# Row gathers moved behind the branch, the first tile's pairs moved ahead, first scores put inside the projections

## What is computed

```python
def rgcn(h, V, w_comp, loop_w, bias, ffn_w, ffn_b, ln_g, ln_b, norm, src, dst, etype):
    Hb = einsum('ni,bio->bno', h, V)                 # 4 bases
    coef = w_comp[etype]
    m = sum(coef[:, b][:, None] * Hb[b][src] for b in range(4)) * norm[:, None]
    agg = segment_sum(m, dst)
    hn = relu(agg + h @ loop_w + bias)
    y = hn @ ffn_w.T + ffn_b + h
    return (y - mean(y)) / sqrt(var(y) + 1e-8) * ln_g + ln_b

def conv(x, src, dst, Wq, bq, Wk, bk, Wv, bv, Ws, bs):   # 2 heads of 64
    q, k, v = x @ Wq + bq, x @ Wk + bk, x @ Wv + bv
    alpha = sum(q[dst] * k[src], -1) / 8
    a = segment_softmax(alpha, dst)
    return segment_sum(v[src] * a, dst) + x @ Ws + bs

x = layernorm(x + rgcn(x, ..., edge_weight, src, dst, edge_type))
x = layernorm(x + conv(relu(conv(x, ...1)), ...2))
```

## Time and profile before

| | us |
|---|---|
| median of 3 runs (range) | 2037.31 (2036.69 to 2038.35) |
| the profiled execution, its own time | 2049.78 |
| its span in the trace | 2047.9 |
| start to the first pair product (L842) | 51.6 |
| second block ends, layer 1 begins | 1078.9 |
| layer 2 begins | 1563.2 |

### The profile page before, as it was taken

The page is one execution under the profiler, slowest core; times in us unless marked ns, Lnnn a source line. Parts: engine busy times, 40 slices in busy tenths (PEclk is TensorE's granted clock), DMA queues, the critical chain, the costliest instruction groups (busy, mean ns, idle before and its releaser), DMA issues. The chain is left out here.

```text
span 2047.9 us, 53122 instructions
## 1 busy us (share of the span) xinstructions
PE 1958.0 (96%) x19165; PEld 1634.9 (80%) x19165; DVE 1438.9 (70%) x4141; ACT 1287.0 (63%) x2275; POOL 663.0 (32%) x802
## 2 busy tenths in 40 slices
PE   1699999999999999999998999999998999999998
PEld 1599999999999999999985777777776677777777
DVE  4787878777887877778635666666664666776665
ACT  1476766767676676767654666666663666666665
POOL 3566576566657656665310000000000000000000
PEclk8799999999999999999999999999999999999999
DMA  3012111111211111121013222222211232222220
GB/s 82 6 38 76 41 39 49 67 39 39 73 44 39 47 69 39 39 73 40 34 66 125 70 91 94 94 93 70 88 63 64 99 103 94 79 98 101 101 101 8
DMA packets 43019, 137.00 MB, mean 67 GB/s; under 512 B 9191, under 2 KB 24360, under 8 KB 36485
## 3 DMA queue, kind: packets, MB, share of 16 engines
q1 hardware_dynamic: 38484, 128.24, 17.5%
q0 software_dynamic: 4400, 6.80, 1.4%
HBM read 91.83 MB, written 43.20 MB: 66 GB/s over the span
## 5 line engine op out<-in xcount | busy, mean ns | idle before, releaser
L854 PE MATMUL ps<-matrixT,x_rows 125*128 125x256 f32 (+1 forms) x2500 | 563.6, 377 | 0.1
L1670 DVE CUSTOM_DVE_ANT_0 scores_l<-ps,bias_rows_l 125x500 f32<-125x500 f32 (+1 forms) x700 | 396.7, 619 | 212.6 <-issue 212.6
L854 PEld LDWEIGHTS ps<-matrixT,x_rows 125*128 125x128 f32 x2500 | 461.3, 190 | 48.5 <-issue 0.2
L1575 ACT COPY weightsT_l<-ps 125x500 f32<-125x500 f32 x400 | 229.7, 575 | 289.0 <-PE ps L1502 288.4
L942 ACT COPY matrixT<-ps 125x500 f32<-125x500 f32 (+2 forms) x800 | 381.8, 658 | 45.8 <-PE ps L842 44.4
L1502 PEld LDWEIGHTS ps<-eye,scores_l 125*125 125x125 f32 x2500 | 287.9, 188 | 118.2 <-issue 105.1
L842 PE MATMUL ps<-high_weights,low_onehot 64*125 64x125 f32 x6300 | 373.9, 274 | 5.2 <-DVE high_weights L722 3.3
L842 PEld LDWEIGHTS ps<-high_weights,low_onehot 64*125 64x125 f32 x6300 | 358.5, 187 | 24.1 <-issue 18.5
L1567 ACT ACTIVATE scores_l<-scores_l,neg_max_l 125x1500 f32<-125x1500 f32 x200 | 318.0, 1594 | 20.6 <-DVE neg_max_l L1705 20.6
L1502 PE MATMUL ps<-eye,scores_l 125*125 125x125 f32 x2500 | 325.2, 281 | 4.0 <-ACT weightsT_l L1575 2.7
L1487 PE MATMUL ps<-kT_l,q_tile_l 64*125 64x500 f32 (+1 forms) x1400 | 319.1, 567 | 6.6 <-DVE chunk_max_l L1670 4.8
(11 more groups left out here) (152 smaller groups left out, 1600.5 us busy)
## 6 DMA issues: line engine op xcount, KB each, us to landing
bias_rows_l<-bias SPq DMA_DIRECT2D x50, 1562.5 KB, 6.6
bias<-bias SPq DMA_DIRECT2D x75, 500.0 KB
x_rows<-in_x SPq DMA_DIRECT2D x1, 1562.5 KB
bias<-bias SPq DMA_DIRECT2D x25, 62.5 KB
x<-x_rows SPq DMA_DIRECT2D x25, 62.5 KB
x_rows_l<-x SPq DMA_DIRECT2D x25, 62.5 KB
out<-rows_l SPq DMA_DIRECT2D x25, 62.5 KB
dst_int<-in_dst SPq DMA_DIRECT2D x1, 402.8 KB
```

The costliest lines, as they stand in the source:

```text
L854: last = nc.tensor.matmul(psG[:, BASES * SPLIT * side:BASES * (SPLIT * side + SIDE[side])], x[:, h, :], MT[side][:, 0:SIDE[side], BASES * ...
L1575: nc.scalar.copy(PT[i][:, 0:cw[c]], psT[i % 3][0:R, 0:cw[c]]).then_inc(z["pa_ok"], 1)
L1670: V.tensor_tensor_reduce(S[par][:, hd, lo:hi], psS[2 * ((par + j) % 2) + hd][0:R, 0:cw[j]], bias[par][0:R, lo:hi], 1.0, FLOOR, ALU.add, AL ...
```

## The change

There are three parts. The gathers of the rows of tiles 0 and 1 leave the first block and stand at the head of GpSimd's list in the second. In step 3 of the second block the second side of tile 0's pair products (and ScalarE's evacuation of it) stands ahead of the turning of tile 1's edge weights instead of behind it. In both attention layers ScalarE evacuates k as well as q; the projections of q and k use PSUM banks 4 to 7, so that banks 0 to 3 are free for scores; tile 0's scores stand between and behind the projections of q and k; and the values come after them, in one row over four banks, with their evacuation on VectorE behind tile 0's masks and negative maximum.

```diff
@@ -284,8 +284,6 @@
                                     pattern=[[-1, 128]], channel_multiplier=1).then_inc(const, 1)
             nc.gpsimd.memset(m["spare"][:, :], 0.0).then_inc(const, 1)
             pool.wait_ge(const, 5)
-            for s in range(EARLY):
-                find_row(nc, pool, a, m, s, s)
 
         @block.tensor
         def _(pe):
@@ -549,6 +547,8 @@
 
         @block.gpsimd
         def _(pool):
+            for s in range(EARLY):
+                find_row(nc, pool, a, m, s, s)
             nc.gpsimd.memset(half_power[:, :], -0.5).then_inc(const, 1)
             pool.wait_ge(const, 1)
 
@@ -890,13 +890,16 @@
                     turn_digits(w + 1, par)
                 if inside(u):
                     sums(u, 1, 3)
+                if w == 0:
+                    pair_products(w, 1)
                 if inside(w + 1):
                     read(u, 3)
                     pe.wait_ge(digitsT_ok, w + 2)
                     turn_codes(w + 1, par)
 
                 if inside(w):
-                    pair_products(w, 1)
+                    if w > 0:
+                        pair_products(w, 1)
                     sums(w, 0, 0)
                 if inside(w + 1):
                     pe.wait_ge(codesT_ok, w + 2)
@@ -991,6 +994,8 @@
                 if inside(u):
                     logs(u, 3)
                     sums_out(u, 1)
+                if is_int(w) and w == 0:
+                    evacuate(w, 1)
                 if inside(w + 1):
                     act.wait_ge(codes_ps, w + 2)
                     turned = psM[:, :].rearrange("p (b n) -> p n b", n=128)
@@ -1000,7 +1005,8 @@
                     last.then_inc(codesT_ok, 1)
 
                 if inside(w):
-                    evacuate(w, 1)
+                    if not is_int(w) or w > 0:
+                        evacuate(w, 1)
                     for piece in range(PIECES):
                         counts_out(w, 0, piece)
                 if is_int(w) and w == 0:
@@ -1375,6 +1381,7 @@
         groups = [(g, min(4, T - g)) for g in range(0, T, 4)]
         cw = widths()
         psS, psT, psO = ps[0:4], ps[4:7], ps[7]
+        psQ = ps[4:8]
         ORDER = (0, 1, 2, 3, 4, 5, 6, 7, 8, 12, 13, 9, 10, 11)
         ON_V, ON_A = (1, 4, 7, 10), (0, 2, 3, 5, 6, 8, 12, 9, 11)
         NT = HEADS * CH
@@ -1423,7 +1430,7 @@
         def _(pool):
             nc.gpsimd.memset(half_power[:, :, :], -0.5).then_inc(z["one"], 1)
             pool.wait_ge(z["one"], 1)
-            pool.wait_ge(z["q_ok"], CH)
+            pool.wait_ge(z["q_ok"], 1)
 
             def lay_q(t, par):
 
@@ -1432,6 +1439,7 @@
                 nc.gpsimd.tensor_copy(q_now[par][:, :], qT[:, bass.ds(t * R, R)]).then_inc(z["q_laid"], 1)
 
             lay_q(0, 0)
+            pool.wait_ge(z["q_ok"], CH)
 
             def step(t, par):
                 if inside(t + 1):
@@ -1447,23 +1455,25 @@
 
         @block.tensor
         def _(pe):
-            for j in range(CH):
+            pe.wait_ge(z["one"], 1)
+
+            def project(j):
+
                 if j >= 2:
                     pe.wait_ge(z["q_ok"], j - 1)
                     pe.wait_ge(z["k_ok"], j - 1)
-                nc.tensor.matmul(ps[j % 2][:, 0:cw[j]], W["q"][:, :], inT[:, CW * j:CW * j + cw[j]], start=True, stop=True).then_inc(z["q_ps"], 1)
-                nc.tensor.matmul(ps[2 + j % 2][:, 0:cw[j]], W["k"][:, :], inT[:, CW * j:CW * j + cw[j]], start=True, stop=True).then_inc(z["kk_ps"], 1)
+                nc.tensor.matmul(psQ[j % 2][:, 0:cw[j]], W["q"][:, :], inT[:, CW * j:CW * j + cw[j]], start=True, stop=True).then_inc(z["q_ps"], 1)
+                nc.tensor.matmul(psQ[2 + j % 2][:, 0:cw[j]], W["k"][:, :], inT[:, CW * j:CW * j + cw[j]], start=True, stop=True).then_inc(z["kk_ps"], 1)
+
+            def values(j):
+
                 g, k = groups[j]
-                if j >= 2:
-                    pe.wait_ge(z["v_ok"], j - 1)
+                if j >= 4:
+                    pe.wait_ge(z["v_ok"], j - 3)
                 for i in range(k):
-                    to = ps[4 + j % 2][0:R, i * D:(i + 1) * D]
+                    to = psQ[j % 4][0:R, i * D:(i + 1) * D]
                     last = nc.tensor.matmul(to, inT[:, (g + i) * R:(g + i + 1) * R], W["v"][:, :], start=True, stop=True)
                 last.then_inc(z["v_ps"], 1)
-            pe.wait_ge(z["q_ok"], CH)
-            pe.wait_ge(z["k_ok"], CH)
-            pe.wait_ge(z["v_ok"], len(groups))
-            pe.wait_ge(z["one"], 1)
 
             def product(u, c):
 
@@ -1479,6 +1489,8 @@
             def scores(t, par, j):
                 if j == 0:
                     pe.wait_ge(z["q_laid"], t + 1)
+                if is_int(t) and t == 0:
+                    pe.wait_ge(z["k_ok"], j + 1)
 
                 if not is_int(t) or t * CH + j >= 2:
                     pe.wait_ge(z["masked"], (t * CH + (j - 2)) * 2 + 2)
@@ -1506,11 +1518,29 @@
                 for i in range(lo, hi):
                     turn(u, up, i)
 
+            def first_step():
+
+                for j in range(CH):
+                    project(j)
+                    if j in (3, 5):
+                        scores(0, 0, j - 3)
+                        scores(0, 0, j - 2)
+                for j in range(4, CH):
+                    scores(0, 0, j)
+                pe.wait_ge(z["q_ok"], CH)
+                for j in range(len(groups)):
+                    values(j)
+
             def step(t, par):
                 u, up, w = t - 1, 1 - par, t - 2
+                if is_int(t) and t == 0:
+                    first_step()
+                    return
                 if inside(t):
                     scores(t, par, 0)
                     scores(t, par, 1)
+                if is_int(t) and t == 1:
+                    pe.wait_ge(z["v_ok"], len(groups))
                 if inside(u):
                     turns(u, up, 0, 3)
                 if inside(w):
@@ -1548,8 +1578,11 @@
             act.wait_ge(z["bq_ok"], 1)
             for j in range(CH):
                 act.wait_ge(z["q_ps"], j + 1)
-                nc.scalar.activation(qT[:, CW * j:CW * j + cw[j]], ps[j % 2][:, 0:cw[j]], ACT.Identity, scale=SCALE,
+                nc.scalar.activation(qT[:, CW * j:CW * j + cw[j]], psQ[j % 2][:, 0:cw[j]], ACT.Identity, scale=SCALE,
                                      bias=bq_scaled[:, :]).then_inc(z["q_ok"], 1)
+                act.wait_ge(z["kk_ps"], j + 1)
+                nc.scalar.activation(kT[:, CW * j:CW * j + cw[j]], psQ[2 + j % 2][:, 0:cw[j]], ACT.Identity,
+                                     bias=bk[:, :]).then_inc(z["k_ok"], 1)
 
             def sums_out(w, par):
                 act.wait_ge(z["pv_ok"], (w + 1) * CH)
@@ -1605,14 +1638,14 @@
             V = nc.vector
             V.memset(qT[:, NODES:NODES + R], 0.0)
             V.tensor_scalar_mul(bq_scaled[:, :], bq[:, :], SCALE).then_inc(z["bq_ok"], 1)
-            for j in range(CH):
-                v.wait_ge(z["kk_ps"], j + 1)
-                V.tensor_scalar_add(kT[:, CW * j:CW * j + cw[j]], ps[2 + j % 2][:, 0:cw[j]], bk[:, :]).then_inc(z["k_ok"], 1)
-                g, k = groups[j]
-                v.wait_ge(z["v_ps"], j + 1)
-                V.tensor_tensor(vals[:, g:g + k, :, :], ps[4 + j % 2][0:R, 0:k * D].rearrange("p (t h f) -> p t h f", h=HEADS, f=HD),
-                                bv.rearrange("p (h f) -> p h f", h=HEADS).unsqueeze(1).to_broadcast([R, k, HEADS, HD]),
-                                ALU.add).then_inc(z["v_ok"], 1)
+
+            def values_out():
+                for j in range(len(groups)):
+                    g, k = groups[j]
+                    v.wait_ge(z["v_ps"], j + 1)
+                    V.tensor_tensor(vals[:, g:g + k, :, :], psQ[j % 4][0:R, 0:k * D].rearrange("p (t h f) -> p t h f", h=HEADS, f=HD),
+                                    bv.rearrange("p (h f) -> p h f", h=HEADS).unsqueeze(1).to_broadcast([R, k, HEADS, HD]),
+                                    ALU.add).then_inc(z["v_ok"], 1)
 
             def finish(w, par, then):
                 v.wait_ge(z["exp_ok"], (w + 1) * 4)
@@ -1703,6 +1736,8 @@
                     if not is_int(t) or t >= 2:
                         v.wait_ge(z["exp_ok"], (t - 1) * 4)
                     V.tensor_scalar_mul(neg[par][:, :], top[:, :], -1.0).then_inc(z["neg_ok"], 1)
+                if is_int(t) and t == 0:
+                    values_out()
                 if inside(u):
                     turned_out(10)
                 if layer == 2 and inside(w):
```

## The result

| | kernel before | changed kernel |
|---|---|---|
| median of 4 runs (range), us | 2037.83 (2036.69 to 2038.86) | 2026.82 (2025.05 to 2030.42) |
| ratio, 95% interval | | 0.9947 (0.9933 to 0.9962) |
| profiled execution, us | 2049.78 | 2030.42 |

The change gives 11 us (8 to 14 by the interval), where 27.7 were forecast; the time lies 10 us above the top of the range. Measured again later, the changed kernel took 2029.32 beside 2037.88, ratio 0.9955 (0.9941 to 0.9968).

A forecast was written before the change was run, and what follows sets the result against it. TensorE was taken as the bound, with time to win only where it waits. Gathers 7.2, second side 8.6 and attention layers 11.9 sum to 27.7 us off 2037.31, giving 2009.6; range 2005.5 to 2016.5, chance 0.59.

The forecast's parts named there:

- every engine's branch and its first instructions move along: End of first block: with the barrier 7.5 us earlier, all engines' starts behind it come earlier too; 7.2 us taken.
- the time that VectorE takes to come out of its branch: Start of second block: this time hides GpSimd's constant ahead of the first wait; VectorE wants first rows at 21.1.
- the barrier stays: Rival, end of first block: drain is the barrier's own time or engines wait for code; gain 0, 2016.8 us, chance 0.04.
- gathers late: Rival, start of second block: moved gathers meet x and weights and land late; gain 3.5 us, 2013.3, chance 0.13.
- after that VectorE waited for TensorE in the old order and has this time to give: Second block after unit 3 of tile 1: VectorE's slack (20% idle) lets TensorE's 8.6 us gain stand.
- Slower: Rival, second block: VectorE, working beside GpSimd's coefs every step, becomes the bound; 55 us lost, 2064.8, chance 0.04.
- nothing in VectorE's row after it is longer than before: Second block after unit 3: argument against the rival that only VectorE's own 2.2 us is won.
- new gaps after 100 us: Sign of being wrong: TensorE shows new gaps in the second block's steps after 100 us.
- VectorE gates: Rival, step 3 of second block: unit 3 or the logarithms come after TensorE; only 2.2 us won, 2016.0, chance 0.08.
- 1.75 for the clock: Start of each attention layer: first projection chunk takes 1.75 us more at the lower clock, counted in old and new order.
- with no waits 6.6 each: Attention layers: upper bound of the reordering's gain, 6.6 us in each layer if TensorE never waits.
- projections worth less: Rival, attention layers: ScalarE's pitch or late bias rows leave 4 us a layer; 2013.5 us, chance 0.11.

The follow-up runs named there:

- part 3 alone: Kernel before with only the attention reordering (scores inside the projections, both layers); 2030.69 us, ratio 0.9965.
- x_late: Changed kernel with SyncE asking for x after all weights, in the second block; one execution, 2040.52 us, total not meaningful since x is late.
- x112: Changed kernel with x loaded as 112 and 13 partitions instead of 125; 2035.83 us beside 2050.9, ratio 0.9930; repeated 2021.44, ratio 0.9925.
- p23_x112: Changed kernel with x loaded as 112 and 13 partitions and the gathers back in the first block; 2035.08 us beside 2050.9, ratio 0.9920.
- best: Changed kernel with x and destination loads split by partitions, four logarithm tiles, bias fills on GpSimd; 2028.87 us beside 2050.9, ratio 0.9895; repeated 2013.88, ratio 0.9884.
- ln4: Changed kernel with four tiles for ScalarE's logarithms, one for each piece, instead of two; 2024.11 us beside 2038.99, ratio 0.9931.
- part 2 alone: Kernel before with only tile 0's second side put ahead of tile 1's weights; 2034.19 us, ratio 0.9981.
- parts 2 and 3: Changed kernel with the row gathers put back in the first block; 2024.24 us, ratio 0.9941 against the kernel before.
- p1_only: Kernel before with only the gathers moved to the second block; 2040.2 us beside 2037.84, ratio 1.0011.
- x_split: Changed kernel with x asked for on two queues, 13 tiles by SyncE and 12 by ScalarE; 2028.21 us beside 2038.99, ratio 0.9946.
- p23_best: Kernel with split x and destination loads, four logarithm tiles and GpSimd's fills, but gathers in the first block; 2015.9 us, ratio 0.989.

## Why the prediction was wrong, point by point

**The forecast's frame held.** TensorE stays busy through the steady steps, and what a start gains arrives at the end: part 3 alone, 7.1 by the medians, 7.7 read off the layers. All three sizes were too large: 27.7 forecast, 9 to 11 measured. The lower bounds missed too: their sum was 13.2, part 1 (3) and part 3 (8) fell below theirs, and only part 2 came out above its 2.2.

**Part 1, forecast 7.2, measured -2.2.** The failed step is "every engine's branch and its first instructions move along". The branch moved; the first instructions did not. The prediction took "the time that VectorE takes to come out of its branch" (5.1 us before, counted from the end of the reading of the flag) as a fixed length, but it is 8.1 us with x in flight and 3.3 to 3.7 without (x_late, x112, p23_x112 and both forms of best). The price lay in the rows: GpSimd issues at 16.0 was put in from 23.54 - 7.5, while x was named only as something that "does not come earlier" and as a risk for the gathers' landing, never for the starts. The rival "the barrier stays" held the right words, "or all engines wait for code", at a chance of 0.04, and argued against only the first half. The rival "gathers late" was right that the landing is the drain's 5.6 us under x, but priced it behind an issue at 19.5 that came at 26.4. Behind the late start the gathers now stand in front, which turned nothing into a loss of 2.2. Even with x out of the way the step gives about 1 us, since it puts issue and landing behind the branch that had run inside the drain.

**Part 2, forecast 8.6, measured 3.9.** Up to the place where the forecast stopped its sum it was right: 9.07 us read (40.56 against 49.63). The failed step is "after that VectorE waited for TensorE in the old order and has this time to give". It priced the units alone. In step 4 VectorE has two fills and four bias rows besides, in the old order too. It comes to the first of them 56.9 us after the first pair product (111.02), where it was 62.6 before (114.27): 5.8 us earlier, while TensorE is 9.1 earlier. The rows that carry this are, in the kernel before,

```profile
103.33 0.55 DVE L717 TENSOR_TENSOR high_weights<-iota,digitsT 128x200 f32<-128x200 f32 x1 [6.00 <-PE ps L842]
...
114.27 0.89 DVE L735 MEMSET bias<- 32x1000 f32 x1 [0.26 <-issue]
```

and in the changed one

```profile
98.03 0.62 DVE L717 TENSOR_TENSOR high_weights<-iota,digitsT 128x200 f32<-128x200 f32 x1
...
111.02 0.89 DVE L735 MEMSET bias<- 32x1000 f32 x1 [0.26 <-issue]
```

VectorE's wait of 6.0 us is used up. And counted from the first pair product it starts on these units 7.8 us earlier (43.87 against 51.69), but loses 2.05 of that before the fill: 12.99 us against 10.94. All three of its units now lie beside GpSimd's `coefs`, where before only the first did and a part of the second: the last unit's two large builds take 1.45 and 1.84 us instead of 1.22 and 0.98. By these rows this is the mechanism of the rival "Slower", for one step, and goes against the prediction's "nothing in VectorE's row after it is longer than before". No run takes it away by itself, so what it costs the kernel is not shown. The two waits behind it are also the prediction's own sign of being wrong, new gaps after 100 us. With two tiles ScalarE's third logarithm waits for that bias row, and TensorE for the logarithm; with the low clock in this execution 5.2 us went back. This is the mechanism of the rival "VectorE gates", one step later than it was put, and its price (2.2 us left) is nearer to the 3.9 than the forecast's. ln4 shows the cause: without it step 4 lasts 40.5.

**Part 3, forecast 11.9, measured 7.1 (7.7 in the profile).** The order did what was said: VectorE's masks come first, values later, and no wait over 0.41 us stands in TensorE's row. The negative maximum comes 22.5 us after the start of the layer (forecast 21, before 28.9). Two terms were mis-sized, and they are the failed step of this part. With the clock full from the start, which is the case in layer 2 of two profiles, the old order takes 34.23 (part 2 alone)

```profile
1549.50 1.08 PE L1460 MATMUL ps<-hT,Wq 128*128 128x500 f32 x2 [0.88 <-PEq L1338]
...
1583.73 1.57 PE L1508 MATMUL ps<-eye,scores_l 125*125 125x125 f32 x12 [0.71 <-ACT weightsT_l L1581]
```

and the new one 29.13 (parts 2 and 3):

```profile
1543.19 1.11 PE L1465 MATMUL ps<-hT,Wq 128*128 128x500 f32 x2 [1.00 <-POOL minus_half_l L1431]
...
1572.32 1.57 PE L1514 MATMUL ps<-eye,scores_l 125*125 125x125 f32 x12
```

Without its 1.75 for the clock the forecast had 28.2 (its bound "with no waits 6.6 each" is a slip, 35.9 - 29.0 gives 6.9), so 0.9 us a layer is missing: the last chunk of 125 columns takes 0.88 for q and k and not 0.42, each change between projections and scores 0.1, the values 5.65 and not 5.5. The other term is the clock. The forecast took the 1.75 us of the old order; in the profile of the changed kernel the low clock costs 31.94 - 29.13 = 2.8 and 3.0 us, in that of the kernel before 1.6 and 1.7. Together 1.9 + 2.3 = 4.2, the 11.9 against 7.7. The first term is the order's; the second I can't ascribe to it: over the profiles of this case the low clock at a layer's start lasted from nothing to 6.3 us, with either order (old order: 4.0 and 4.5 before, 3.0 and 3.75 in p1_only, 5.25 and none in p2_only; new order: 5.75 and 6.25 in the changed kernel, 5.0 and 5.75 in its repetition, 4.0 and none in p3_only and in p23). What decides it stays open. The rival "projections worth less" had the size, 4 a layer, by another cause: ScalarE's evacuations held nothing up (0.16 us between two).

**The span.** Taking the gain off the median was right, though for a reason the forecast didn't know: the 12.5 us between them belong to that execution and not to the kernel.

## What to carry to other kernels

When a barrier falls earlier, ask what each engine needs to start behind it, and what is in flight then: here a large load delayed VectorE's first operation and GpSimd's first gather by 4 to 5 us. A wait that hides a landing is not a gain until the landing has another cover. When an engine's idle time is taken away in one step, follow its row through the next step with all that stands in it, not only with what was moved, and with what another engine now does beside it. And look at the DMA share beside the rate: x at 95 GB/s with a share of 0.38 was a transfer on a few engines, and cutting its 125 partitions into 112 and 13 was worth 6 to 8 us, as much as the best of the three parts (7.1).

## What the runs showed of the hardware that was not expected

The time from the end of the reading of the flag at the branch to VectorE's first operation is 8.1 us with x in flight and 3.5 without (x_late; 3.3 to 3.7 in the kernels with x split by partitions). The issue of the first weight by SyncE takes 7.63 us behind the whole of x on its queue, and 0.41 in x_late and x_split. A GpSimd gather of 141 KB lands 2.0 to 2.2 us after the end of its issue when the queues are quiet (p23_best, p23_x112), 5.6 us beside x. VectorE, from its first build for unit 4 to its first fill, takes 12.99 us beside GpSimd's `coefs` in the changed kernel and 10.94 in the kernel before. And TensorE's clock at the start of the same layer, or behind the same waits in step 4, was low in some executions and full in others.
